# A four-layer gated cross-attention stack on one core: the order of 661 stage instances, from fixed strides to a table of single places

## What is computed

```python
x = x + tanh(g_xattn[0]) * L0_xattn(layernorm(x), ctx, ctx)      # gated linear attention, 8 heads, group norm
x = x + tanh(g_ffn[0])   * L0_ffn(layernorm(x))                  # 8 experts, top 2, capacity 320, gelu(a) * g
x = x + tanh(g_xattn[1]) * L1_xattn(layernorm(x), ctx)           # x @ W1 + mean(ctx) @ W2 + b
x = x + tanh(g_ffn[1])   * L1_ffn(layernorm(x))                  # quantised FFN: four maxima over the whole tensor
x = x + tanh(g_xattn[2]) * L2_xattn(layernorm(x), ctx)           # masked self attention, cross attention, FFN, 3 norms
x = x + tanh(g_ffn[2])   * L2_ffn(layernorm(x))                  # 8 experts, top 2, silu(gate) * up
x = x + tanh(g_xattn[3]) * L3_xattn(layernorm(x), ctx, ctx)      # 16-head cross attention
x = x + tanh(g_ffn[3])   * L3_ffn(layernorm(x))                  # 8 small experts and a shared one
```

## Time and profile before

| | |
|---|---|
| median of 3 runs | 561.14 us (558.23, 561.46, 561.14) |
| profiled execution: span, first to last instruction | 556.3 us (the profile gives no other time for it) |
| mean granted PE clock | 0.855 of full speed |
| PE / weight loads / DVE / ACT / POOL busy | 75% / 48% / 70% / 58% / 45% |
| instructions | 11344 |

### The profile page before, as it was taken

The page is one execution under the profiler, slowest core; times in us unless marked ns, Lnnn a source line. Parts: engine busy times, 40 slices in busy tenths (PEclk is TensorE's granted clock), DMA queues, the critical chain, the costliest instruction groups (busy, mean ns, idle before and its releaser), DMA issues. The chain is left out here.

```text
span 556.3 us, 11344 instructions
## 1 busy us (share of the span) xinstructions
PE 414.8 (75%) x4098; PEld 267.4 (48%) x4113; DVE 389.7 (70%) x1061; ACT 320.6 (58%) x664; POOL 252.5 (45%) x415
## 2 busy tenths in 40 slices
...
GB/s 216 184 35 2 0 1 111 179 1 2 2 1 2 1 0 0 0 0 2 2 2 1 3 2 2 2 2 2 0 1 1 2 2 2 2 1 2 1 20 19
DMA packets 26003, 11.28 MB, mean 20 GB/s; under 512 B 16359, under 2 KB 22877, under 8 KB 25949
## 3 DMA queue, kind: packets, MB, share of 16 engines
...
...
## 5 line engine op out<-in xcount | busy, mean ns | idle before, releaser
L642 POOL TENSOR_TENSOR work<-work 128x512 f16<-128x512 f32 x64 | 73.9, 1176 | 54.4 <-ACT work L1142 54.3
L546 POOL TENSOR_SCALAR vr<-mv 128x1 f32<-128x1 f32 x88 | 19.1, 218 | 144.5 <-DVE mv L1295 143.7
L1081 ACT ACTIVATE phase<-psum 128x1024 f16<-128x1024 f16 (+2 forms) x60 | 50.9, 861 | 32.4 <-PE psum L693 13.7
L1678 DVE TENSOR_REDUCE qs<-psum 128x4 f16<-128x512 f32 x96 | 59.5, 687 | 8.2 <-PE psum L966 8.0
L1195 ACT ACTIVATE work<-psum 128x512 f32<-128x512 f32 x64 | 37.2, 594 | 35.3 <-PE psum L862 32.7
L875 PE MATMUL psum<-wout,work 128*128 128x128 f16 x768 | 48.6, 220 | 9.9 <-POOL work L642 7.0
L548 POOL TENSOR_TENSOR rstd<-vr,mhalf 128x1 f32<-128x1 f32 x88 | 49.6, 563 | 7.3
L875 PEld LDWEIGHTS psum<-wout,work 128*128 128x128 f16 x768 | 44.9, 98 | 16.6 <-POOL work L642 9.4
L860 PE MATMUL psum<-zTh,split 128*128 128x512 f16 x128 | 51.0, 398 | 2.1 <-POOL zTl L647 1.6
L1254 ACT ACTIVATE phase<-psum 128x512 f32<-128x512 f32 x96 | 50.0, 627 | 2.7 <-PE psum L693 2.2
L1142 ACT ACTIVATE work<-work 128x512 f16<-128x512 f32 x64 | 38.3, 629 | 22.3 <-DVE work L1570 21.7
...
## 6 DMA issues: line engine op xcount, KB each, us to landing
...
```

The source lines that it names most:

```text
L642: ch.do(pool.tensor_tensor(hidl[:, n % 2, k, :], act[:, n % 2, k, :], hidh[:, n % 2, k, :], ALU.subtract), sem("hid_low"))
L1081: ch.do(A(out, view(u), ACT.Copy), banks.freed(stage, b, name))
L1678: ch.do(v.tensor_reduce(groups(qs[:, b, :, 3 * DA:3 * DA + 1], 4)[:, j], u, AX.X, ALU.max, negate=True), free_of(stage, b, f"s{j}"))
```

## The change

`START`, `PERIOD` and `GAP` are replaced by `PLACE`, which gives each of the 661 instances a place of its own, 1 to 661. `CHAINS` and the stages' code stay. Two buffers become pairs, used in turn: `nrm` and `rden`. One wait is added in x0_split (DVE waits for its own `x0_z` of that batch, since that may now stand directly before). No arithmetic, no DMA and no PSUM rule is changed; the instances are the same 661, and ACT loads its tables 15 times in both.

```diff
-START = {
-    "x0_norm": -6.97, "x0_z": -3.11, "x0_t": -1.76, "x0_gate": -0.54,
...
-PERIOD = {"n0": 1.0, "s0": 0.79, "w8": 1.35, "x0": 1.0, "s2": 1.11, "f0": 1.5,
-          "so": 0.5, "x1": 0.16, "u1": 0.62, "x2": 1.26, "f2": 1.5, "x3": 1.44}
+PLACE = {
+    "x0_norm": [1, 2, 3, 4, 5, 6, 7, 8], "x0_z": [9, 10, 11, 13, 19, 20, 21, 24],
...
-                place = START[name] + turn * PERIOD.get(phase, 0.0) + half * GAP.get(phase, 0.0)
-                steps.append((place, -s, name, item))
+        items = [item for item, _, _ in ITEMS.get(phase, [(0, 0, 0)])]
+        for name in names:
+            steps += [(place, name, item) for place, item in zip(PLACE[name], items)]
...
-        nrm = sb("nrm", [P, H0])
+        nrm = sb("nrm", [P, 2, H0])
...
-        rden = sb("rden", [P, HA])
+        rden = sb("rden", [P, 2, HA])
...
+                    dve.wait_ge(sem("x0_z"), b + 1)
                     twice(qq[:, :, 0:2 * D0].rearrange("p h (s d) -> p h s d", d=D0), zb, H0)
...
-                    ch.do(stt(nrm[:, :], nrm[:, :], 1e-5, nrm[:, :], ALU.mult, ALU.mult))
+                    ch.do(stt(nrm[:, b % 2, :], nrm[:, b % 2, :], 1e-5, nrm[:, b % 2, :], ALU.mult, ALU.mult))
...
-                    r = rden[:, :].rearrange("p (j g) -> p j g", j=4)
+                    r = rden[:, back_turn[stage, b] % 2, :].rearrange("p (j g) -> p j g", j=4)
```

More of the change, by code:

```diff
@@ L77 @@
 }
-START = {
-    "x0_norm": -6.97, "x0_z": -3.11, "x0_t": -1.76, "x0_gate": -0.54,
-    "x0_forget": 13.47,
-    "split0": 18.08,
-    "w1": 27.14,
-    "w8_scale": 33.17, "w8_units": 34.17, "w8_whole": 35.17, "w8_back": 36.17, "w8": 37.77,
-    "x0_split": 12.8, "x0_stack": 13.8, "x0_score": 14.8, "x0_value": 15.8, "x0_back": 16.8, "x0_group": 17.8,
-    "f0_z": 18.8, "f0_t": 20.98,
-    "f0_route": 28.53, "f0_count": 30.49,
-    "router": 35.4, "scale_rows": 67.96,
-    "split2": 95.59,
-    "f0_up": 28.5, "f0_cut": 29.11, "f0_down": 31.03,
-    "split_out": 55.96,
-    "x1_norm": 42.9, "x1_z": 44.44, "x1_t": 45.19, "x1_out": 46.01, "f1_z": 46.96, "f1_t": 48.1,
-    "f1_scale": 72.88,
-    "f1_up": 72.91,
-    "f1_gate": 76.74, "f1_prod": 78.7, "f1_out": 79.67,
-    "f1_down": 90.28, "x2_z": 91.56, "x2_t": 92.59, "a_kv": 93.59, "a_stack": 94.59, "a_max": 95.67,
-    "a_again": 97.09, "a_exp": 98.02, "a_av": 99.59, "b_kv": 101.09, "a_back": 101.6, "a_wt": 102.09, "a_wo": 103.09,
-    "a_norm": 104.09, "b_qt": 105.09, "b_q": 106.15, "b_stack": 107.03, "b_max": 108.13, "b_again": 109.63,
-    "b_exp": 110.63, "b_av": 112.15, "b_back": 112.9, "b_wt": 113.56, "b_wo": 114.33, "b_norm": 115.56, "b_ft": 116.56,
-    "b_f": 117.56, "b_last": 118.45, "f2_z": 119.49, "f2_t": 120.49,
-    "f2_route": 124.35,
-    "f2_up": 125.93, "f2_cut": 126.78, "f2_down": 128.53,
-    "x3_norm": 142.4, "x3_z": 143.4, "x3_t": 144.20000000000002, "c_kv": 145.4, "c_stack": 146.4, "c_max": 147.3,
-    "c_again": 148.9, "c_exp": 149.8, "c_av": 151.35, "c_back": 152.1, "c_wt": 152.8, "c_wo": 153.9, "f3_z": 154.9,
-    "f3_t": 155.9,
-    "f3_route": 161.65, "f3_up": 162.5, "f3_gt": 165.43, "f3_gate": 166.0, "f3_down": 167.20000000000002, "f3_back": 168.3,
-}
@@ L120, in schedule @@
     for phase, names in CHAINS.items():
-        for s, name in enumerate(names):
-            for item, turn, half in ITEMS.get(phase, [(0, 0, 0)]):
-                place = START[name] + turn * PERIOD.get(phase, 0.0) + half * GAP.get(phase, 0.0)
-                steps.append((place, -s, name, item))
-    return [("setup", 0)] + [(name, item) for _, _, name, item in sorted(steps, key=lambda step: step[:2])]
+        items = [item for item, _, _ in ITEMS.get(phase, [(0, 0, 0)])]
+        for name in names:
+            steps += [(place, name, item) for place, item in zip(PLACE[name], items)]
+    return [("setup", 0)] + [(name, item) for _, name, item in sorted(steps, key=lambda step: step[0])]
 UNITS = {
@@ L450, in gated_stack @@
         back_users = [(s, b) for s, b in order if s in ("a_back", "b_back", "c_back")]
+        back_turn = turns("a_back", "b_back", "c_back")
         pt_users = [(s, b) for s, b in order if s in ("a_av", "b_av", "c_av")]
```

24 lines of the change are left out of this document (21 added, 3 removed), and 25 rows, old and new, of the table PLACE.

## The result

The changed kernel takes 509.1 us (median of 4 runs, 507.1 to 514.3); the kernel before took 559.7 in the runs beside it (4 runs, 554.9 to 561.5). The ratio is 0.917 with an interval of 0.913 to 0.922: **8.3% faster**. I had forecast 545 and a range of 533 to 557. The direction was right, the size was not, and the time lies outside the range. Spans of the two profiled executions: 556.3 and 512.6 us, so the forecast of -16 stands against -43.7 there, and against -50.6 in the medians: the profiled execution of the changed kernel was the longest of its four (514.3).

What follows compares the result with a forecast made beforehand. It took no single engine as the bound (PE, the busiest, at 75%), so order and waits could matter. The terms summed to -16 us on a 556.3 us span, 540.3, and with 4.8 added 545 us; range 533 to 557.

Steps and rivals of the forecast that it cites:

- A: End of layer 0's attention: less time from DVE's last product to the last normalising, -4.5 us.
- B: Layer 0's attention: three fewer split0 residues on POOL ahead of the last score, -2 us, ends 0 and -5.6.
- C: Start of layer 0's experts: f0_up 0/0 ahead of the last three transposes, route starts sooner, -2 us, ends 0 and -2.8.
- F: Quantised FFN: residues on POOL and the rows' scaling delay DVE's serial chain, +2.5 us, ends 0 and +9.3.
- H: Into layer 2's experts: f2_up 0/0 stands 11 places earlier, -2 us, ends +2 and -4.4.
- Rival 1: Gains given back as early batches wait at a full PE or for a bank: 554.6 or 556.6 us; chance 0.13.
- rival 2: Three batch loops: ragged order makes PE stop for readers of banks, slower, 577 or 569 us; chance 0.08.
- rival 3: Quantised FFN: POOL blocks the serial chain of DVE, 553 us, 556.5 at worst; chance 0.14.
- G: First attention of layer 2: seven of eight split2 steps leave, PE sets the pace, -1.5 us, ends 0 and -4.5.
- D: Layer 0's experts: last f0_down 12 places earlier, some steps behind it, PE near full, -1.5 us, ends 0 and -8.
- I: Last stretch: f3_up 0 behind c_exp 7, c_wo 7 ahead of f3_down 0, -5 us, ends -1 and -7.
- rival 4: All favourable ends of the terms reached half way: -28 us, 533 us; chance 0.12.

Runs made afterwards that it cites:

- e10: Order of before with both buffers doubled, only the steps up to f0_cut 0 in the change's order; 550.2 us, 0.985 of the kernel before.
- e3: Order of before with both buffers doubled, f1_down to the last f2_t in the change's order, split2 behind its old neighbours; 537.6 us, ratio 0.970.
- e4: Order of before with both buffers doubled, only the steps behind the last f2_t in the change's order; 542.7 us, 0.977 of the kernel before.
- e1: The changed kernel's program with both buffers doubled but every step at its place of before; 556.4 us, 1.000 of the kernel before.
- e2: As e1, with only the eight split2 steps moved to the change's places; 561.7 us, 1.010 of the kernel before.
- e13: The changed kernel run again, unedited; 507.7 us, 0.914 of the kernel before.
- e14: The changed kernel with split2 put back behind its old neighbours; 511.0 us, 0.920 of the kernel before.
- e17: As e1, with layer 0's experts, the w8 steps and layer 1's norms up to f1_scale in the change's order, run for its trace; 548.7 us.
- e18: As e1, with only c_exp 7 moved ahead of f3_up 0 and c_wo 7 ahead of f3_down 0; 553.5 us, 0.994 of the kernel before.
- e8: As e1, with only the last 42 steps, from place 620 on, in the change's order; 549.8 us, 0.988 of the kernel before.

## Why the prediction was wrong

**A, B, C and F were right.** Their measured sum is -6.1 against -6.0, and e10 shows that the first three reach the end. H is near its -2 only in the profiled execution; by the other traces it is about -5, past its end of -4.4, most of it in PE's busy time. Rival 1 (gains given back at a full PE) is refuted by that, rival 2 (a ragged order is slower in the ring of banks) by e3 and e4, and rival 3 by F's +3.2, though its mechanism is there and costs 2.3 us in four instructions. (Rival 3's worst case, -3.4, gives 557.7 by my own sum, not the 556.5 that I wrote.)

**The step that failed is G**, in the words "PE sets the pace and idles 4.5". It was read from 266 to 322, the middle of the attention, where PE is busy 92% of the time. Most of the attention's end, with its recurring meetings, lies outside it: e1 has three waits of PE for DVE from 313 us on, 3.2 us. The whole attention idles 9.9 us in e1. Worse, I took busy time as work. Of e3's 12.4 us 6.5 are idle time and 5.9 are busy time that vanished (73.4 to 67.5), 3 of it by the clock. A PE that is 88% busy at 0.94 was bounded by me at its idle share; it gave back more than that. And the term was only for the seven splits that leave. These are worth nothing in the old order (e2) and 2.3 us of the stretch in the new one (e13 against e14), not far from the -1.5. For the new order of the attention's own steps, 12.4 us in e3, I had no term at all.

**The same in D and in the third attention.** D's upper end, -8, held the -6.1, but I took -1.5, with "PE is near full and its list's products are the same"; e17 shows four waits for one residue turned into one. The third attention's loop I costed at nothing and gave no reason; its steps moved by up to 15 places. In the earlier trace rows its stretch from 505 to 535 has a clock of 0.84, and 336 to 400 one of 0.82: I read these and did not ask what order had to do with them. I itself was near (e18: -3.6 for the two moves, forecast -5; e8, with all of the last 42 steps, -6.5). One price in it swings without any edit: f3_down 0's eight products take 3.70 us in the trace of before and 5.40 in e1's, which has the same order, 3.70 in the changed kernel's and 5.33 in e13's.

**What I had called the sign of my error** was that the loops costed at nothing would move, and they did. I gave -28, rival 4, a chance of 0.12 as all favourable ends half way; all of them in full give -39.1, and the truth, -43.7, is past even that: the ends themselves were too narrow.

**Open.** By what means the order raises the granted clock, since it also falls behind stretches in which PE was hardly idle (e4 at 514); where the 3 us of e3's attention lie that are neither clock nor gaps; whether ACT or POOL makes the splits dear in the new order; what the 2.0 us of "issue" in e17 is.
